# Weaving a quantized feed-forward part into the attention loop, sequence by sequence, with silu written as tanh

## The reference

```python
x = x + tanh(g_xattn[0]) * _L0_xattn_ref(_layernorm(x), ctx, ctx, ...)
x = x + tanh(g_ffn[0])   * _L0_ffn_ref(_layernorm(x), w_gate, w_up, w_down)
x = x + tanh(g_xattn[1]) * _L1_xattn_ref(_layernorm(x), ctx, ctx, ..., 16)
x = x + tanh(g_ffn[1])   * _L1_ffn_ref(_layernorm(x), ...)
# _L0_ffn_ref, 128 -> 512 -> 128:
_act_quant(x):    scale = 127 / clip(max|x| of the token, 1e-5); round(x * scale) / scale
_weight_quant(w): scale = 1 / clip(mean|w|, 1e-5); clip(round(w * scale), -1, 1) / scale
_bitlinear(x, w): _act_quant(x) @ _weight_quant(w).T
y = _bitlinear(silu(_bitlinear(x, w_gate)) * _bitlinear(x, w_up), w_down)
```

## Time and profile before

| | us |
|---|---|
| median of 3 runs (180.66 to 180.68) | 180.67 |
| the profiled execution | 180.67 |
| its span, first to last instruction | 178.9 |
| PE busy | 165.0 |
| DVE busy | 126.0 |
| ACT busy | 83.7 |
| POOL busy | 54.7 |

### The profile page before, as it was taken

How to read it: one execution, slowest core, us unless ns; L and a number is a source line. 1 busy time by engine, 2 the same in 40 slices (tenths; PEclk the granted TensorE clock), 3 DMA queues, 4 the chain that set the end, 5 groups by cost and what they waited for, 6 DMA issues and landing times.

```text
span 178.9 us, 3936 instructions
## 1 busy us (share of the span) xinstructions
PE 165.0 (92%) x1530; PEld 105.9 (59%) x1538; DVE 126.0 (70%) x341; ACT 83.7 (47%) x154; POOL 54.7 (31%) x91
## 2 busy tenths in 40 slices
PE   7998999999999998888597799999999998999993
PEld 5644546665455454466365676647577665666672
DVE  0579365779779879698988698659838494654453
ACT  2255775654664655768566951365230313212210
POOL 8635652267884723436023005200002000000000
PEclk9999999999999999999999999999999999999999
DMA  5986000000000000000000000000000000100001
GB/s 157 395 297 286 0 0 5 4 2 4 2 4 4 0 4 0 0 4 2 0 4 0 0 0 4 0 2 0 2 4 0 0 0 0 59 4 0 0 0 59
DMA packets 1890, 5.83 MB, mean 33 GB/s; under 512 B 208, under 2 KB 592, under 8 KB 1744
## 3 DMA queue, kind: packets, MB, share of 16 engines
q1 hardware_dynamic: 1152, 4.01, 6.2%
q10 hardware_dynamic: 720, 1.57, 2.4%
HBM read 5.06 MB, written 0.52 MB: 31 GB/s over the span
## 4 chain that ended last, share of the span: by engine, by line
PE 68%; DVE 16%; ACT 7%; POOL 4%; issue 3%; POOLq 0%; DVEq 0%
PE banks L1342 10%; PE banks L1367 10%; PE banks L1345 10%; PE banks L1132 8%; DVE banks L748 4%; PE banks L1124 3%; PE banks L1178 3%; PE banks L1181 2%; POOL vz L264 2%; ACT ffn_work L536 2%; PE banks L1355 2%; ACT f_hqT L542 2%; PE banks L1162 2%; PE banks L1036 2%; PE banks L1152 2%
## 5 line engine op out<-in xcount | busy, mean ns | idle before, releaser
L748 DVE TENSOR_REDUCE banks<-banks 128x8 f32<-128x1024 f32 x16 | 19.7, 1230 | 10.8 <-PE banks L1132 10.8
L302 POOL TENSOR_SCALAR_AFFINE_SELECT pT<-pT 128x512 f32<-128x512 f32 x32 | 19.9, 644 | 24.2 <-ACT pT L459 24.1
L1367 PEld LDWEIGHTS banks<-ews,rest 128*128 128x128 f32 x160 | 20.6, 191 | 7.8 <-issue 7.7
L1036 PE MATMUL banks<-idle 128*128 128x256 bf16 x158 | 23.0, 293 | 1.2 <-DVE idle L659 1.2
L636 ACT ACTIVATE full<-banks 128x512 f32<-128x512 f32 x20 | 11.9, 593 | 21.9 <-PE banks L1342 21.9
L459 ACT ACTIVATE pT<-banks 128x512 f32<-128x512 f32 x32 | 17.3, 594 | 8.7 <-PE banks L1162 8.6
L1367 PE MATMUL banks<-ews,rest 128*128 128x128 f32 x160 | 21.0, 275 | 0.0
L1342 PE MATMUL banks<-nT,ews 128*128 128x512 f32 x40 | 20.6, 597 | 0.2
L994 DVE TENSOR_TENSOR xnT<-full,banks 128x512 f32<-128x512 f32 x20 | 13.7, 683 | 9.6 <-PE banks L1345 7.3
L1345 PE MATMUL banks<-nT,ews 128*128 128x512 f32 x40 | 20.4, 592 | 0.0
L1036 PEld LDWEIGHTS banks<-idle 128*128 128x128 bf16 x158 | 16.4, 105 | 5.2 <-DVE idle L659 1.2
(11 more groups left out here) (170 smaller groups left out, 287.7 us busy)
## 6 DMA issues: line engine op xcount, KB each, us to landing
ews<-in_ew SPq DMA_DIRECT2D x1, 1928.5 KB, 7.3
fws<-in_fw SPq DMA_DIRECT2D x1, 768.0 KB, 8.1
cT<-in_ctxT ACTq DMA_DIRECT2D x2, 256.0 KB, 5.3
x_all<-in_x SPq DMA_DIRECT2D x2, 256.0 KB, 4.7
lws<-in_lw ACTq DMA_DIRECT2D x1, 449.0 KB, 8.4
sels<-in_sel ACTq DMA_DIRECT2D x1, 320.0 KB, 8.7
a<-in_aw ACTq DMA_DIRECT2D x1, 256.0 KB, 5.1
out_x<-x_all SPq DMA_DIRECT2D x1, 256.0 KB, 2.0
```

What stands on the lines that cost most here:

```text
L302: nc.gpsimd.affine_select(out=probs, in_=probs, compare_op=ALU.is_ge, fill=0.0, base=0, pattern=[[0, HG], [1, S]], channel_multiplier=-1). ...
L748: V.tensor_reduce(bank[2 * p][:, 0:2 * HG], banks[p][:, :].rearrange("p (h k) -> p h k", h=2 * HG), AX.X, ALU.max).then_inc(sm["a_mx"], 1)
L1036: mm(bank[t][:, 0:2 * S], idle[:, 0:128], idle[:, :], start=True, stop=True)
L1367: last = mm(bank[t][:, b * D:(b + 1) * D], e_h[:, u, b * S:(b + 1) * S], expert(c)[2], start=(c == 0 and (b == 0 or s == 1 and b == 2)), s ...
```

## The change

Layer 0's feed-forward part is no longer a stage behind the loop. Sequence m is normalized, quantized and multiplied inside the passes m + 2 to m + 5 of the attention loop; in pass n the loop holds `gate_up(n-3)`, `hidden(n-3)`, `h_transposes(n-4)`, `down(n-5)`. What is left over behind the loop (`gate_up` for 5, 6 and 7, and what follows them) is put among layer 1's attention of half 0.

Other work per sequence than before: POOL computes rstd for one sequence at a time and normalizes it (`x_prepare`; before, DVE did it for half 0, POOL for half 1). DVE finds the maximum and the scale of 128 columns (`x_steps`), ACT scales and rounds (`x_scaled`), PE transposes in f32, ACT copies (`xqT_copy`), POOL computes the two factors that undo the scales (`x_dequant`). silu(g) = 0.5 g (1 + tanh(0.5 g)): ACT takes the tanh of the gate (`gate_tanh`), adds one (`tanh_plus_one`) and copies the scaled up part out of PSUM (`up_copy`), POOL multiplies these two (`gated_up`), DVE multiplies by the gate in PSUM (`hidden`). Before, ACT took the silu and DVE did one product of three factors. Two loads of activation tables behind the loop go (one for silu, one for exp).

Gate and up each have one bank now (5 and 4), and bank 4 also takes both transposes and the result of `down`. The weights' quantization and the second half's projections move one or two passes ahead; `half1_masked(2)` and `(3)` stand in pass 3 behind `max_copy(3, 1)`; POOL's `own_tokens` stand in passes 2 to 5, behind `x_dequant`. POOL also normalizes layer 1's half 1 (n3), which DVE did.

Behind the loop, the lists are, in this order. DVE: `aggregate(1, 0)`, `residual(6)`, `layer_stats(6)`, `hidden_steps(4)`, `hidden(5)`, `layer1_normalize(0)`, `heads_out(7)`, `x_steps(6)`, `ffn_residual(4)`, `residual(7)`, `layer_stats(7)`, `hidden_steps(5)`, `softmax3_args(0)`, `hidden(6)`, `x_steps(7)`, `ffn_residual(5)`, `softmax3_normalize(0)`, `hidden_steps(6)`, `hidden(7)`, `residual3(0)`, `ffn_residual(6)`, `hidden_steps(7)`, `layer1_normalize` of n4, `ffn_residual(7)`. PE, without its `keep_busy` matmuls (60 of them up to there, 111 before): `down(4)`, `keys_times_queries(0)`, `values_times_outputs(0)`, `scores3_bias(0)`, `x3_transposes(0)`, `y_proj(7)`, `xq_transpose(6)`, `scores3(0)`, `gate_up(6)`, `h_transposes(5)`, `down(5)`, `xq_transpose(7)`, `keys_times_queries(1)`, `gate_up(7)`, `p3_transposes(0)`, `values_times_outputs(1)`, `h_transposes(6)`, `y3_proj(0)`, `down(6)`, `h_transposes(7)`, `down(7)`, `x4_transposes(0)`. ACT: for 5, 6 and 7 tanh, plus one, up copy, each followed by `hidden_scale` and `hT_copy` of the sequence before; `hidden_scale(7)`, a load of the silu table, `hT_copy(7)`. POOL: `bias_into_x(0)`, `x_prepare(7)`, `gated_up(6)`, `x_dequant(7)`, `gated_up(7)`, `rstd_of(2, 0)`, `rstd_of(1, 1)`, the normalization of n3's half 1.

The new functions and the loops (POOL, ACT, DVE, PE in this order; indentation and blank lines reduced):

```diff
+def x_prepare(m):
+    pool.wait_ge(sm["q_mv"], m + 1)
+    nc.gpsimd.tensor_scalar(ve[:, m:m + 1], mv[:, 2 * m + 1:2 * m + 2], EPS, None,
+                            ALU.add).then_inc(sm["q_ve"], 1)
+    pool.wait_ge(sm["q_ve"], m + 1)
+    nc.gpsimd.tensor_tensor(rstd[:, m:m + 1], ve[:, m:m + 1], mhalf[:, m:m + 1],
+                            ALU.pow).then_inc(sm["q_rstd"], 1)
+    pool.wait_ge(sm["q_rstd"], m + 1)
+    nc.gpsimd.tensor_scalar(tok(f_xn, m), tok(x_all, m), mv[:, 2 * m:2 * m + 1], rstd[:, m:m + 1],
+                            ALU.subtract, ALU.mult).then_inc(sm["q_xn"], 1)
+def x_dequant(m):
+    pool.wait_ge(sm["q_step"], XSTEPS * m + 2)
+    pool.wait_ge(sm["w_clip"], 1)
+    nc.gpsimd.tensor_scalar(f_deq[:, 0, m:m + 1], f_a[:, 1, m:m + 1], fclip[:, 0:1], 0.5,
+                            ALU.mult, ALU.mult).then_inc(sm["q_deq"], 1)
+    pool.wait_ge(sm["q_deq"], 2 * m + 1)
+    nc.gpsimd.tensor_scalar(f_deq[:, 1, m:m + 1], f_a[:, 1, m:m + 1], fclip[:, 1:2],
+                            f_deq[:, 0, m:m + 1], ALU.mult, ALU.mult).then_inc(sm["q_deq"], 1)
+def gated_up(m):
+    u = m % 2
+    pool.wait_ge(sm["f_t1"], m + 1)
+    pool.wait_ge(sm["f_us"], m + 1)
+    if m >= 2:
+        pool.wait_ge(sm["f_hr"], m - 1)
+    nc.gpsimd.tensor_tensor(f_p[:, u, :], f_sil[:, u, :], f_up_s[:, u, :], ALU.mult).then_inc(sm["f_pr"], 1)
...
-    elif n == 3:
-        own_tokens(0, 0)
-    elif n == 4:
-        own_tokens(1, 0)
+    elif n == B - 1:
+        rstd_of(1, 0)
     causal(n, 2)
     causal(n, 3)
-    if n == 2:
+    if n >= 1:
+        x_prepare(n - 1)
+    if n >= 2:
+        gated_up(n - 2)
+    if n >= 1:
+        x_dequant(n - 1)
+    if n == 0:
+        nc.gpsimd.memset(wT[:, :], 0.0).then_inc(sm["wT_zero"], 1)
+    elif n == 1:
         spread_values(1)
+    elif n == 2:
+        own_tokens(0, 0)
     elif n == 3:
+        own_tokens(1, 0)
+    elif n == 4:
         own_tokens(0, 1)
-    elif n == 4:
+    elif n == 5:
         own_tokens(1, 1)
-    elif n == 5:
-        rstd_of(1, 0)
...
+def x_scaled(m):
+    act.wait_ge(sm["q_step"], XSTEPS * m + 3)
+    nc.scalar.activation(tok(f_t, m), tok(f_xn, m), ACT.Identity, scale=f_a[:, 2, m:m + 1],
+                         bias=magic[:, 0:1]).then_inc(sm["q_xs"], 1)
+def xqT_copy(m):
+    act.wait_ge(sm["f_xqTp"], m + 1)
+    nc.scalar.activation(f_xqT[:, bass.ts(m, S)], bank[4][:, 0:S], ACT.Identity,
+                         bias=magic[:, 1:2]).then_inc(sm["f_xqTs"], 1)
+def gate_tanh(m):
+    u = m % 2
+    act.wait_ge(sm["f_gp"], m + 1)
+    act.wait_ge(sm["q_deq"], 2 * m + 2)
+    if m >= 2:
+        act.wait_ge(sm["f_pr"], m - 1)
+    nc.scalar.activation(f_sil[:, u, :], bank[5][:, :], ACT.Tanh,
+                         scale=f_deq[:, 0, m:m + 1]).then_inc(sm["f_th"], 1)
+def tanh_plus_one(m):
+    u = m % 2
+    act.wait_ge(sm["f_th"], m + 1)
+    nc.scalar.activation(f_sil[:, u, :], f_sil[:, u, :], ACT.Identity,
+                         bias=ones_sq[:, 0:1]).then_inc(sm["f_t1"], 1)
+def up_copy(m):
+    u = m % 2
+    act.wait_ge(sm["f_up"], m + 1)
+    if m >= 2:
+        act.wait_ge(sm["f_pr"], m - 1)
+    nc.scalar.activation(f_up_s[:, u, :], bank[4][:, :], ACT.Copy,
+                         scale=f_deq[:, 1, m:m + 1]).then_inc(sm["f_us"], 1)
...
+for n in range(B):
+    if n:
+        exp(n - 1, 2)
+        exp(n - 1, 3)
+        if n >= 3:
+            gate_tanh(n - 3)
+        max_copy(n, 0)
+        if n >= 3:
+            tanh_plus_one(n - 3)
+            up_copy(n - 3)
+    if n == 1:
+        xT_copy(1)
+        weights_scaled(0)
+    elif n == 2:
+        weights_out(0)
+        weights_scaled(1)
+    elif n >= 4:
+        hidden_scale(n - 4)
+        if n == 4:
+            weights_out(2)
+    exp(n, 0)
+    exp(n, 1)
+    if n >= 4:
+        hT_copy(n - 4)
+    max_copy(n, 1)
+    if n == 0:
+        k_copy(1)
+        weights_abs(1)
+        weights_abs(2)
+    elif n == 1:
+        q_copy(1)
+        v_copy(1)
+        half1_masked(0)
+    elif n == 2:
+        layer1_copy(0)
+        weights_out(1)
+        half1_masked(1)
+        layer1_copy(1)
+    elif n == 3:
+        half1_masked(2)
+        half1_masked(3)
+    if n >= 2:
+        x_scaled(n - 2)
+        xqT_copy(n - 2)
+    if n == 3:
+        weights_scaled(2)
+exp(B - 1, 2)
+exp(B - 1, 3)
...
+def x_steps(m):
+    at = lambda k: XSTEPS * m + k
+    dve.wait_ge(sm["q_xn"], m + 1)
+    V.tensor_reduce(f_a[:, 0, m:m + 1], tok(f_xn, m), AX.X, ALU.max,
+                    apply_absolute_value=True).then_inc(sm["q_step"], 1)
+    dve.wait_ge(sm["q_step"], at(1))
+    V.tensor_scalar(f_a[:, 1, m:m + 1], f_a[:, 0, m:m + 1], QMIN, 1.0 / 127.0, ALU.max, ALU.mult)\
+        .then_inc(sm["q_step"], 1)
+    dve.wait_ge(sm["q_step"], at(2))
+    V.reciprocal(f_a[:, 2, m:m + 1], f_a[:, 1, m:m + 1]).then_inc(sm["q_step"], 1)
+def hidden(m):
+    u = m % 2
+    dve.wait_ge(sm["f_gp"], m + 1)
+    dve.wait_ge(sm["f_pr"], m + 1)
+    if m >= 2:
+        dve.wait_ge(sm["f_htr"], m - 1)
+    V.tensor_tensor(f_h[:, u, :], bank[5][:, :], f_p[:, u, :], ALU.mult).then_inc(sm["f_hr"], 1)
+def hidden_steps(m):
+    u = m % 2
+    at = lambda k: STEPS2 * m + k
+    dve.wait_ge(sm["f_hr"], m + 1)
+    V.tensor_reduce(f_ah[:, m, 0:1], f_h[:, u, :], AX.X, ALU.max,
+                    apply_absolute_value=True).then_inc(sm["f_hstep"], 1)
+    dve.wait_ge(sm["f_hstep"], at(1))
+    V.tensor_scalar(f_ah[:, m, 1:2], f_ah[:, m, 0:1], QMIN, 1.0 / 127.0, ALU.max, ALU.mult)\
+        .then_inc(sm["f_hstep"], 1)
+    dve.wait_ge(sm["f_hstep"], at(2))
+    V.reciprocal(f_ah[:, m, 2:3], f_ah[:, m, 1:2]).then_inc(sm["f_hstep"], 1)
+    dve.wait_ge(sm["w_deq"], 1)
+    V.tensor_scalar(f_ah[:, m, 3:4], f_ah[:, m, 1:2], fdown[:, 0:1], None,
+                    ALU.mult).then_inc(sm["f_hstep"], 1)
+def ffn_residual(m):
+    dve.wait_ge(sm["f_yp"], m + 1)
+    dve.wait_ge(sm["f_hstep"], STEPS2 * (m + 1))
+    V.scalar_tensor_tensor(tok(x_all, m), bank[4][:, 0:D], f_ah[:, m, 3:4], tok(x_all, m),
+                           ALU.mult, ALU.add).then_inc(sm["f_res"], 1)
+    dve.wait_ge(sm["f_res"], m + 1)
+    V.bn_stats(tok(stats, m, 6), tok(x_all, m)).then_inc(sm[f"ln_stats{m // HALF}"], 1)
...
-        layer_stats(n - 2, (n - 2) // HALF)
-    if n == 2:
+        layer_stats(n - 2)
+    if n == 1:
         weight_scales()
-    elif n == 3:
-        q_masked(1, 1)
-        q_masked(1, 3)
-    elif n == 5:
-        aggregate(1, 0)
-        weights_clipped(0)
-    elif n == 6:
-        weights_clipped(2)
+    elif n == 2:
+        weights_clipped(1)
+    elif n >= 4:
+        hidden_steps(n - 4)
+        if n == 4:
+            weights_clipped(2)
     top(n, 1)
     split_max(n, 1)
+    if n >= 3:
+        hidden(n - 3)
     if n:
         heads_out(n - 1)
+    if n >= 2:
+        x_steps(n - 2)
+    if n >= 4:
+        ffn_residual(n - 4)
     if n == 0:
         normalize_half(1)
+    elif n == 1:
+        weights_clipped(0)
     elif n == 2:
         q_masked(1, 0)
+        q_masked(1, 1)
     elif n == 3:
         q_masked(1, 2)
-    elif n == 5:
-        weights_clipped(1)
...
+def xq_transpose(m):
+    pe.wait_ge(sm["q_xs"], m + 1)
+    if m:
+        pe.wait_ge(sm["f_us"], m)
+    else:
+        pe.wait_ge(sm["proj_out"], J_RAW + 2)
+    if m >= 2:
+        pe.wait_ge(sm["f_res"], m - 1)
+    nc.tensor.transpose(bank[4][:, 0:S], tok(f_t, m), ident).then_inc(sm["f_xqTp"], 1)
+def gate_up(m):
+    pe.wait_ge(sm["f_xqTs"], m + 1)
+    if m == 0:
+        pe.wait_ge(sm["w_q"], 2)
+    else:
+        pe.wait_ge(sm["f_th"], m)
+        pe.wait_ge(sm["f_hr"], m)
+    mm(bank[5][:, :], f_xqT[:, bass.ts(m, S)], fq[:, 0, :], start=True, stop=True).then_inc(sm["f_gp"], 1)
+    mm(bank[4][:, :], f_xqT[:, bass.ts(m, S)], fq[:, 1, :], start=True, stop=True).then_inc(sm["f_up"], 1)
+def h_transposes(m):
+    u = m % 2
+    pe.wait_ge(sm["f_htr"], m + 1)
+    pe.wait_ge(sm["f_us"], min(m + 2, B))
+    if m:
+        pe.wait_ge(sm["f_res"], m)
+    for c in range(4):
+        last = nc.tensor.transpose(bank[4][:, c * S:(c + 1) * S],
+                                   f_ht[:, u, c * 128:(c + 1) * 128], ident)
+    last.then_inc(sm["f_hTp"], 1)
+def down(m):
+    u = m % 2
+    pe.wait_ge(sm["f_hTs"], m + 1)
+    if m == 0:
+        pe.wait_ge(sm["w_q"], 3)
+    for c in range(4):
+        last = mm(bank[4][:, 0:D], f_hqT[:, u, c * S:(c + 1) * S], fq[:, 2, c * D:(c + 1) * D],
+                  start=(c == 0), stop=(c == 3))
+    last.then_inc(sm["f_yp"], 1)
...
 for n in range(1, B):
     score_masks(n, 0)
+    if n >= 5:
+        down(n - 5)
     max_rows(n - 1, 1)
     scores(n, 0)
     transposed_scores(n - 1, 1)
     if n >= 2:
         y_proj(n - 2)
+    if n >= 3:
+        xq_transpose(n - 3)
     subtract_max(n - 1, 1)
+    if n >= 3:
+        gate_up(n - 3)
     heads(n - 1, 0)
     if n == 1:
         x_transposes(1)
+        weight_sums()
     elif n == 2:
-        v_proj(1)
-        weight_sums()
-    elif n == 3:
```

(11 more changed lines are left out.)

464 lines of the change are left out of this document (137 added, 327 removed).

## The result

The change makes the kernel slower: 196.62 us (196.28 to 196.87, the profiled execution apart) against 180.67, a ratio of 1.088 with a 95% interval of 1.086 to 1.090. The forecast was 190.4 with a range of 184 to 196: right in direction and in the main on the mechanism, too low by 6.2 us and outside its range.

The account below looks back on a forecast made before the run. The prediction took a ring through POOL to bound the woven loop: 17.3 + 68.6 (loop) + 35.4 (tail) = 121.4, 9.8 later than 111.6; span 178.9 + 9.8 = 188.7, plus 1.8 around it, gives 190.4 us, range 184 to 196.

Parts of the forecast that it names:

- the ring through POOL: In the loop, POOL's work and DVE's `hidden`, `heads_out`, `x_steps` wait on each other; 10.2 us per pass with `own_tokens`.
- the pieces: Durations summed for a loop pass, such as four `causal` 2.4, `x_prepare` 1.6, `gated_up` 1.27, `own_tokens` 1.5; 9.7 us.
- the experts' stage: Behind `x4_transposes(0)`: the change touches nothing PE waits for, so 67.3 us stay as they are.
- PE's clock: Gaps in each pass could lower it partly to 1.2 GHz, giving over 200 us; chance 0.03, otherwise priced at nothing.
- the loop: Passes 1 to 7 sum to 68.6 us from 17.32, so it ends at 86.0, 18.3 later than before.
- the tail: From the loop's end to `x4_transposes(0)`: four distances of 9.4, 9.3, 7.6 and 9.1, 35.4 us against 43.9 before.
- Loop, passes 1 to 3: The loop's first three laid-out passes, forecast to take 8.8, 8.6 and 9.3 us.
- second ring: Loop path from `x_steps` by `gate_up`, `heads`, masks and ACT's steps to `gated_up`, `hidden`, `heads_out`; 8.7 us per pass.
- the added 0.5: In a loop pass, `heads(N-1, 1)` stands behind `h_transposes` and `hidden_scale`, so `heads_out` waits some 0.5 us more.
- The rival of dear one-column operations: POOL's one-column operations cost 1.1 us more in each of five passes, the power 1.05 in some; 196 us, chance 0.13.
- `scores(4, 0)` behind `half1_masked(3)`: In pass 4 of the loop, a wait of some 1.9 us on PE, helping make that pass 11.3.
- The rival "faster": POOL hides wholly and PE bounds the loop; passes 3 to 7 must average 8.3 or less; 178.5 us, chance 0.09.

Follow-up runs that it names:

- e3_xfirst: Changed kernel with `x_steps` moved ahead of `hidden` and `heads_out` in DVE's list; 189.92 us, ratio 1.049.
- e5_poolhalf: e1_fill with fewer idle matmuls and half the columns of POOL's `gated_up` product left out (wrong values); 194.56 us, ratio 1.077.
- e1_fill: Changed kernel with idle matmuls put where PE waits, nothing else; 195.18 us, ratio 1.080.
- e7_masked: e1_fill with `half1_masked(2)` and `(3)` one pass earlier, `weights_clipped(1)` behind `top(2, 1)`, 14 idle matmuls ahead of `scores(4, 0)` gone; 194.75 us.
- e12_tailonly: e1_fill's loop with e10_tail's tail (own banks, order, `scores3_bias(1)` ahead of `x4_transposes(0)`); 188.25 us, ratio 1.040.
- e8_experts: e4_all with `scores3_bias(1)` again ahead of `x4_transposes(0)` and n3's second half normalized by DVE again; 186.22 us, ratio 1.031.
- e9_actorder: e8_experts with ACT's `up_copy` and `tanh_plus_one` ahead of `max_copy(n, 0)`, and two idle matmuls, not eight, ahead of `h_transposes`; 184.52 us.
- e11_order: e10_tail's order of all lists, but sequences 6 and 7 again in the shared banks 4 and 5; 182.57 us, ratio 1.009.
- e10_tail: e9_actorder with another tail: own banks for sequence 6, another for sequence 7's x, layer 1's half 0 and `x_steps(6)` earlier; 179.36 us.
- e4_all: Changed kernel with `own_tokens` ahead of `x_dequant`, `x_steps` ahead of `hidden`, four single moves, and idle matmuls in remaining waits; 186.81 us.

## Why the prediction came out as it did

**What failed.** The direction, the ring through POOL and the pieces were right. The steps that failed are two terms put at nothing: the experts' stage ("the change touches nothing in them that PE waits for", 67.3 us; measured 68.8) and PE's clock ("with nothing in this trace for it"; 1.4 to 1.8 us). The rest is size: at a full clock the loop is 1.9 longer than forecast and the tail 1.0. 190.4 + 1.5 + 1.9 + 1.0 + 1.8 = 196.6, the measured time. Without the two terms at nothing the forecast would have been 193.3 to 193.7, in its range.

**Loop, passes 1 to 3** (forecast 8.8, 8.6, 9.3): 8.83, 8.32 and 9.57 in the changed kernel. Right, each within 0.3.

**The ring through POOL** (forecast 10.2 for passes 5 to 7): it exists, and breaking it at `x_steps` (e3_xfirst) is the largest gain. The sum was 0.3 low for a pass, but one link of it was wrong. The prediction closed the ring by `gated_up`, `hidden`, `heads_out`; e5_poolhalf shows that the product could be 0.5 shorter with no effect. The ring closes through PE: `causal`, `heads`, masks, row maxima, three steps of ACT, `h_transposes`, `heads`. That is the end of the prediction's second ring joined to the start of its first. The first part, `heads_out` to the end of the second `causal`, was forecast as 4.9 and is 5.2 (67.72 to 72.90, where the second head group starts). For the second part two `causal` 1.2, `x_prepare` 1.6, the product 1.27, `hidden` 0.65 and the added 0.5 stood in the sum, 5.2, where PE and ACT take 5.3: near by chance, though not by much of one, since the path by POOL's product ends only some 0.3 earlier. (The second ring's terms sum to 8.5, not the 8.7 that the prediction states; nothing hangs on it.) The added 0.5, for `heads(N-1, 1)` behind `hidden_scale`, was this link, priced as a remainder.

**The pieces**: the power of one column took 0.57 (taken as 0.4), `x_dequant` 0.26 and 0.34 (forecast 0.55 together), `own_tokens` 1.52, `causal` 2.42, the product 1.27. Right. The rival of dear one-column operations (196) gave about the measured time, but not by its mechanism: at 0.57, 0.26 and 0.34 they are cheap.

**Terms that were mis-sized.** Against e1_fill's profiled execution (195.56, span 193.8) the forecast of 190.4 is short by 5.1:
- The loop ends at 88.6 and not 86.0. Passes 3 and 4 take 22.6 together where the forecast had 20.6 (23.0 in the changed kernel, part of pass 4 at half clock). Of these 2.0, 0.8 is the low clock in pass 3; the other 1.2 are sizes. Passes 5 to 7 take 0.3 more each. Pass 4's ring is longer by 0.4 for `x_dequant` (0.53 and 0.46 there). The forecast had `scores(4, 0)` behind `half1_masked(3)` as a reason for the long pass 4; that wait was there (1.72), but e7_masked takes it away and the pass stays at 12.2: it lay beside POOL's chain. What else makes up pass 4's excess stays open.
- The tail takes 36.4 (88.6 to 125.0) and not 35.4. Its four distances, by the starts of `hidden` at 98.18, 107.98 and 115.77, are 9.6, 9.8, 7.8 and 9.3, forecast as 9.4, 9.3, 7.6 and 9.1.
- "Behind it 67 us as before" failed outright: 68.8. The change moves `scores3_bias(1)` from ahead of `x4_transposes(0)` to behind `hidden_proj(2)`, which the prediction does not mention, and gives n3's second half to POOL, which it prices at nothing without naming what would hide it. Before, the matmul stood where PE was not full (32.62 of 39 us); among the experts it has no such place (62.94 of 67), and its return gives 0.9 (e12_tailonly). With the normalization back on DVE too, e8_experts has 1.4 back.
- The clock: held for a risk of 3 in 100 with over 200 us. It came in part: 1.4 us in the medians (196.62 against 195.18), 1.8 against e1_fill at a full clock, and more in the profiled execution, where it is half in four stretches. The prediction had seen that PE would wait 1 to 2 us in each pass and priced the clock at nothing or in full.

**Why slower than before at all.** By e1_fill, the loop lost 20.9 us (67.7 to 88.6), the tail gave back 7.5 (43.9 to 36.4), and the experts' stage lost 1.5: 14.9, the difference of the spans. In pass 6 of the changed kernel PE is busy 8.27 of 10.52 us (68.11 to 78.63), against all of 6.6 before: some 1.7 more of work and 2.3 of waiting. e9_actorder shows that most of the waiting is the order's: with the rings open a pass is 8.8, and PE has 7.85 of 8 us busy (windows of e11_order, which has the same loop, 68 to 76). Some 0.8 us of such a pass are its six idle matmuls, so the work in it is about the 8.1 that the prediction gave a pass bound by PE. And e10_tail shows that the tail was not the work's length either: part of it was the lists' order, part three sequences through one bank for gate and one for up.

**The rival "faster"** (178.5) asked for passes 3 to 7 of 8.3 or less. That point was drawn for a tail of 35.4. e10_tail reaches 179.36 with passes 3 to 7 of 9.0 on the mean (34.50 to 79.66) and a tail of 29.8. The prediction treated the tail as given.

## What to carry to other kernels

When work is woven into a loop, follow each engine's list once round and sum the ring that closes; then look for small producers (here three instructions of 0.15 to 0.3 us) that stand behind large ones for which the next engine waits. Moving those few ahead gave 6.7 us in the medians; leaving out half of a product gave 0.6, and a whole step of ACT 2.9. Work that is moved "for free" must have its cover named: among the experts, where PE was busy 62.94 of 67 us, a matmul of 1.0 cost 0.9. And a stage of latency chains can be cut in two ways: taking five of eight sequences out of this tail gave back 7.5 us, and another order with banks of its own for one of the three that were left gave 5.2 more. Last, read the clock row of every trace before lengths are compared: here executions of one kernel (e1_fill) differ by 0.8 us, the low clock in one pass.

## What the runs showed of the hardware

- POOL's power took 1.05 for four columns and 0.57 for one: by these two an estimated 0.4 fixed and 0.16 for each column.
- A cast of 128x68 on DVE took 1.15 and not 0.20 while POOL ran an addition that it had begun first (e4_all, above), and an addition of 128x4 1.08 and not 0.17 (e10_tail, above). In pass 4 POOL's `x_dequant` in turn took 0.53 and 0.46 and not 0.26 and 0.34, while DVE ran `q_masked`.
- The granted clock fell to half (1.2 GHz) behind waits of PE of 1 to 3 us. In the changed kernel's tail, the windows of the waits and of what followed:

```profile
106.00:110.00 4.00, 1.89 (x16) 1.20 (x14) 1.83 (x6) 3.24 (x6) 1.57 (x2) 0.98 0.00 0
110.00:117.00 7.00, 6.29 (x23) 3.91 (x24) 3.87 (x10) 3.57 (x7) 0.76 (x3) 0.52 0.01 2
...
121.00:124.00 3.00, 0.20 (x2) 0.00 (x0) 2.86 (x15) 0.65 (x1) 1.28 (x2) 0.91 0.00 0
124.00:130.00 6.00, 5.79 (x29) 4.67 (x30) 1.49 (x8) 2.22 (x4) 1.23 (x2) 0.50 0.00 0
```

PE had 1.89 of 4 us and 0.20 of 3 us busy, and then ran at 0.52 and 0.50. With idle matmuls in the waits (e1_fill) its mean was 0.99 to 1.00. Executions of one kernel differ in this: by their mean clock, two of e1_fill's four had one low stretch (0.991) and two had none (1.0).
